# Splitting a product off the end of a recurrence block and running it in the first slots of the attention block behind it

## What is computed

```python
x = _layernorm(x + _L0_attn_ref(...))      # local attention and class token
x = _layernorm(x + _L0_xattn_ref(...))     # causal and cross attention
x = _layernorm(x + _L0_ffn_ref(...))       # expert choice, 16 experts
x = _layernorm(x + _L1_attn_ref(...))      # recurrence, then a gated feed-forward
x = _layernorm(x + _L1_xattn_ref(x, ctx, ctx, ...))  # cross attention, 16 heads
x = _layernorm(x + _L1_ffn_ref(...))       # top 2 of 8 experts

# the end of _L1_attn_ref, x being the residual behind the recurrence:
xn2 = _rmsnorm(x, g_ffn)
hid = _linear(xn2, w_fc, b_fc) * _silu(_linear(xn2, w_fcact, b_fcact))   # 128 -> 512
return x + _linear(hid, w_out, b_out)                                     # 512 -> 128
```

## Time and profile before

| | us |
|---|---|
| three runs | 580.11, 572.04, 574.46 |
| their median | 574.46 |
| the profiled execution, time of the run | 571.62 |
| the same execution, span from first to last instruction | 569.9 |

### The profile page before, as it was taken

One profiled execution on the slowest core, in us unless ns is written; L12 is line 12 of the kernel. 1 busy time (PEld: TensorE's weight loads), 2 busy tenths in 40 slices (PEclk: granted clock), 3 DMA queues, 4 the chain that ended last, 5 costly groups with the idle time before them and its releaser, 6 DMA issues. The chain is left out here.

```text
span 569.9 us, 10425 instructions
## 1 busy us (share of the span) xinstructions
PE 470.7 (83%) x3785; PEld 232.4 (41%) x3832; DVE 372.7 (65%) x868; ACT 223.3 (39%) x451; POOL 186.6 (33%) x310
## 2 busy tenths in 40 slices
PE   3899899988979889885069998697799888999993
PEld 2445444433334333332026986254233333444441
DVE  7555766877677677823996474854478784466574
ACT  1313444445754656673002122332114667624220
POOL 7752639467344471333200005720542100000000
PEclk9999999989998999998579999899699999999998
DMA  7230103054441220007013040000321100250700
GB/s 240 72 96 12 49 2 104 21 178 138 144 106 49 58 56 3 2 3 294 0 39 112 2 168 2 0 1 1 85 56 37 48 3 3 67 157 2 222 18 19
DMA packets 26900, 38.03 MB, mean 67 GB/s; under 512 B 3649, under 2 KB 19521, under 8 KB 26465
## 3 DMA queue, kind: packets, MB, share of 16 engines
q1 hardware_dynamic: 26848, 37.36, 21.8%
HBM read 23.91 MB, written 0.59 MB: 43 GB/s over the span
## 5 line engine op out<-in xcount | busy, mean ns | idle before, releaser
L1093 DVE TENSOR_REDUCE nmax<-bank 128x2 f32<-128x512 f32 (+2 forms) x240 | 144.4, 624 | 79.6 <-PE bank L862 37.9
L974 ACT ACTIVATE arena<-bank 128x512 f32<-128x512 f32 (+2 forms) x256 | 130.9, 526 | 122.6 <-PE bank L866 84.7
L862 PE MATMUL bank<-arena 62*128 62x256 bf16 (+2 forms) x512 | 86.0, 257 | 11.8 <-DVE nmax L1093 5.0
L504 PE MATMUL bank<-causal_qk,identb 128*128 128x512 bf16 x232 | 71.1, 402 | 26.1 <-DVE moe_top L1436 16.0
L866 PE MATMUL bank<-arena 64*128 64x256 bf16 (+2 forms) x512 | 85.8, 256 | 2.2 <-ACT arena L974 1.5
L907 PE MATMUL bank<-arena 128*32 128x256 f32 (+4 forms) x1088 | 73.0, 347 | 9.3 <-POOL arena L729 2.8
L862 PEld LDWEIGHTS bank<-arena 62*128 62x128 bf16 x512 | 29.8, 94 | 77.5 <-issue 46.6
L504 PEld LDWEIGHTS bank<-causal_qk,identb 128*128 128x128 bf16 x275 | 23.8, 104 | 55.7 <-DVE moe_top L1436 15.7
L729 POOL TENSOR_SCALAR_AFFINE_SELECT arena<-arena 128x256 f32<-128x256 f32 x64 | 25.6, 410 | 48.8 <-ACT arena L974 48.0
L866 PEld LDWEIGHTS bank<-arena 64*128 64x128 bf16 x512 | 30.3, 94 | 16.6 <-ACT arena L974 6.5
L907 PEld LDWEIGHTS bank<-arena 128*32 128x32 f32 x1088 | 21.4, 109 | 34.2 <-issue 19.1
(11 more groups left out here) (296 smaller groups left out, 813.5 us busy)
## 6 DMA issues: line engine op xcount, KB each, us to landing
arena<-arena SPq DMA_DIRECT2D x96, 128.0 KB, 2.4
fcw<-in_fc1T SPq DMA_DIRECT2D x16, 256.0 KB, 3.3
arena<-in_fc2T SPq DMA_DIRECT2D x1, 4096.0 KB, 12.5
arena<-comb_rows SPq DMA_DIRECT2D x16, 256.0 KB, 4.3
fcw<-in_last SPq DMA_DIRECT2D x1, 2304.0 KB, 8.3
arena<-pos_rows SPq DMA_DIRECT2D x16, 128.0 KB, 3.0
arena<-comb_rows SPq DMA_DIRECT2D x16, 128.0 KB, 4.3
w<-in_w SPq DMA_DIRECT2D x1, 1216.0 KB, 6.1
```

The lines of the kernel that those rows point to most:

```text
L504: nc.tensor.matmul(bank[:, :], m.identb[:, :], m.causal_qk[:, 0:4, :], start=True, stop=True)
L862: mins = t.matmul(mout[:, i, :], stack_rows(m, nm, h0 + i, 0, MAX_ROWS)[:, qt * P:(qt + 1) * P], stack_rows(m, nm, h0 + i, 1, MAX_ROWS)[:, ...
L974: s.activation(m.prob[h % 8][:, 0:w], score_bank(n, h)[:, 0:w], ACT.Exp).then_inc(exps, 1)
L1093: v.tensor_reduce(m.nmax[n % 2][:, qt, h0:h0 + nh], MX[c % NMX][:, 0:nh * (k1 - k0)].rearrange("p (h k) -> p h k", h=nh), AX.X, ALU.max, n ...
```

## The change

The product of the second half leaves the recurrence. `product_first` stands behind unit 4 in place of `product(0)` behind unit 5. DVE takes the sum and the statistics of the first half behind `hidden(4)` (`spread_first`), its norm behind `hidden(5)` (`norm_first`), and `hidden(6)` and `hidden(7)` last. The transposes of the first half go into bank 0 instead of bank 2. The table of Exp is loaded in the attention block, in slot 4. `hid[1]` moves to columns 12288 to 14335 of `arena`, where it survives into the attention block. There `LastNorm` issues the product of the second half on PE in slot 1, DVE's sum and statistics in slot 4 instead of 0 (behind `split_first`), POOL's power in slot 6 instead of 1, DVE's norm in slot 9 instead of 4, and PE's transposes in slot 14 instead of 10, so that ACT copies them in slot 15 instead of 11.

```diff
-S_NORMED, S_NEEDED = 10, 32 - PRE
+S_PRODUCT, S_SUMMED, S_POWER, S_NORM, S_NORMED, S_NEEDED = 1, 4, 6, 9, 14, 32 - PRE
...
-    hid = [a[:, 14336:16384].rearrange("p (f t) -> p f t", f=FT), a[:, 8192:10240].rearrange("p (f t) -> p f t", f=FT)]
+    hid = [a[:, 14336:16384].rearrange("p (f t) -> p f t", f=FT), a[:, 12288:14336].rearrange("p (f t) -> p f t", f=FT)]
...
         unit(4)
+        product_first()
         unit(5)
-        product(0)
         unit(6)
         unit(7)
-        product(1)
         pe.wait_ge(zf, 1)
         for i in range(4):
-            ins = t.transpose(B[2][:, i * P:(i + 1) * P], m.x[1][:, i, :], m.ident[:, :])
+            ins = t.transpose(B[0][:, i * P:(i + 1) * P], m.x[1][:, i, :], m.ident[:, :])
...
-        act.wait_ge(neg, 3)
-        s.activation(table[:, :], ndt[:, :], ACT.Exp).then_inc(neg, 1)
...
-        for u in range(1, 2 * FT):
+        for u in range(1, FT + 1):
             hidden(u)
+        spread_first()
+        hidden(FT + 1)
         norm_first()
+        for u in range(FT + 2, 2 * FT):
+            hidden(u)
...
     def gpsimd(self, pool, slot):
         m = self.m
-        if slot == 1:
+        if slot == S_POWER:
             pool.wait_ge(self.var_ready, 1)
...
     def tensor(self, pe, slot):
         m = self.m
+        if slot == S_PRODUCT:
+            for i in range(4):
+                for f in range(FT):
+                    ins = self.nc.tensor.matmul(m.bank[1][:, i * D:(i + 1) * D], self.hid[:, f, i * P:(i + 1) * P],
+                                                m.w_out[:, f, :], start=(f == 0), stop=(f == FT - 1))
+            ins.then_inc(self.out_mm, 1)
...
     def scalar(self, act, slot):
         m = self.m
+        if slot == S_SUMMED:
+            self.nc.scalar.activation(self.table[:, :], m.eps[:, 0:1], ACT.Exp).then_inc(self.exp_in, 1)
...
-        if slot == 0:
+        if slot == S_SUMMED:
+            dve.wait_ge(self.out_mm, 1)
...
-        if slot == S_SPLIT + 1:
+        if slot == S_NORM:
             dve.wait_ge(self.rstd_ready, 1)
```

More of the change, by code:

```diff
@@ L1102, in layer0_attention @@
         rec = recurrence(nc, m, dram, ctx)
+        m.late_hid = rec.hid[1]
         choice = expert_choice(nc, m, dram, ctx, rec)
@@ L1588, in recurrence @@
     scaled_in, factors, zeroed = sem("scaled_in"), sem("factors"), sem("zeroed")
-    part.xn_ready = xn_ready
+    part.xn_ready, part.hid = xn_ready, hid
     def tiles(c):
@@ L1662, in unit, with product_first @@
             t.matmul(B[k + 1][:, :], m.w_act[:, f * P:(f + 1) * P], xnT[:, cols(c)], start=True, stop=True).then_inc(ffn_mm, 1)
-        def product(c):
-            pe.wait_ge(hid_in, FT * (c + 1))
+        def product_first():
+            pe.wait_ge(hid_in, FT)
             for i in range(4):
                 for f in range(FT):
-                    ins = t.matmul(B[c][:, i * D:(i + 1) * D], hid[c][:, f, i * P:(i + 1) * P],
+                    ins = t.matmul(B[0][:, i * D:(i + 1) * D], hid[0][:, f, i * P:(i + 1) * P],
                                    m.w_out[:, f, :], start=(f == 0), stop=(f == FT - 1))
@@ L1734, in scalar_on @@
             silu(u)
-        act.wait_ge(neg, 3)
-        s.activation(table[:, :], ndt[:, :], ACT.Exp).then_inc(neg, 1)
         act.wait_ge(xt_mm, 1)
-        s.copy(m.xT[1][:, cols(0)], B[2][:, :]).then_inc(xt_in, 1)
+        s.copy(m.xT[1][:, cols(0)], B[0][:, :]).then_inc(xt_in, 1)
     def vector_on(dve):
@@ L1798, in norm_first @@
             v.tensor_scalar(m.veps[:, tiles(0)], m.mv[:, tiles(0), 1], LN_EPS, None, ALU.add).then_inc(var_ready, 1)
+        def norm_first():
             dve.wait_ge(rstd_ready, 1)
@@ L1827, with __init__ @@
 class LastNorm:
-    def __init__(self, nc, m):
-        self.nc, self.m = nc, m
+    def __init__(self, nc, m, hid):
+        self.nc, self.m, self.hid = nc, m, hid
+        self.table = m.sb("late_table", [P, 1])
         sem = lambda n: m.ctx.enter_context(nc.semaphore("late_" + n))
         self.uses = [(S_NORMED, "normed", 0)]
-        self.var_ready, self.rstd_ready, self.z_ready = sem("var_ready"), sem("rstd_ready"), sem("z_ready")
+        self.var_ready, self.rstd_ready, self.z_ready, self.out_mm, self.exp_in = [sem(n) for n in (
+            "var_ready", "rstd_ready", "z_ready", "out_mm", "exp_in")]
     def sync(self, sp, slot):
@@ L2204, in build @@
         router = Router(nc, m, last, ctx)
-        layer1_cross(nc, m, router, LastNorm(nc, m), Top2(nc, m, last, router))
+        layer1_cross(nc, m, router, LastNorm(nc, m, m.late_hid), Top2(nc, m, last, router))
 def kernel(**inputs):
```

2 lines of the change are left out of this document (1 added, 1 removed).

## The result

The changed kernel takes 572.12 us in the median (569.55 to 577.81, 20 runs), the kernel before 574.81 us (571.52 to 580.73, 20 runs). The ratio of the two is 0.9954 with a 95% interval of 0.9932 to 0.9976: 0.46% or 2.6 us faster, between 1.4 and 3.9 us. The profiled execution of the changed kernel has a span of 567.8 us instead of 569.9, which is 2.1 us less. In the terms of the prediction this is "within 2%", with a gain that is nevertheless clear.

What follows compares the result with a forecast made beforehand. The prediction took the wait chain through PE's late-half transposes to bound the kernel. 6.35 us gained ahead of t0, less 2.65 + 1.65 = 4.3 lost behind it, left about 2.05 us: 571.0 us, range 567.0 to 575.5.

Steps and rivals of the forecast that it cites:

- the footing: Base time for the gain: between the profiled execution (571.62 us) and the median shown (574.46), giving a forecast of 571.0 us.
- Ahead of t0: End of the recurrence: earlier first-half product and norm bring the attention block forward from 396.95 to 390.6 us, 6.35 us gained.
- t0: Start of the first product of the attention block on PE; 396.95 us in the kernel before.
- The split: DVE's split in the attention block, now ahead of the sum: ends at t0 + 5.5 us, clear of POOL's residual.
- The product behind t0: Second half's product on PE in the attention block: starts at t0 + 1.14, takes 3.84 us, ends at t0 + 4.98.
- The norm: DVE's four late-half tile norms: each waits for about one POOL instruction, 3.15 us instead of 1.50, 1.65 us lost.
- its upper end: Norm's worst case: POOL waits as well, a whole POOL instruction lies between any two norms, 2.4 us lost.
- Transposes: PE's transposes of the late half: start at t0 + 12.55 us; 8.24 us behind it before.
- The clock, costed at nothing: PE's clock around transposes and fillers: no change if it rises at the same filler, otherwise about 2 us either way.
- the clear norm: Rival: the late half's norm meets no POOL instruction; loss 2.65 us, gain 3.7 us, 569.3 us; chance 0.25.
- the gain absorbed: Rival: something else holds the first maxima, such as stacking DMAs or a later wait; gain 0, 573 us; chance 0.1.
- The slow product: Rival: clock falls at the seam, the moved product takes 7.5 instead of 3.84 us; 1.1 us loss, 574.1 us; chance 0.15.

Runs made afterwards that it cites:

- The run with the late product: The changed kernel with the second half's product behind the queries of job 1 (slot 10) instead of in slot 1; ratio to the kernel before 0.9990.
- the run in which POOL waits: The changed kernel, but POOL waits for the late half's norm before the residual of job 0 and split of job 1; ratio to the kernel before 0.9936.
- the one in which only the residual meets the norm: The changed kernel with the late half's transposes in slot 10 instead of 14, ACT's copy ahead of job 1's high part; ratio to the kernel before 0.9937.
- the run that left one of 6.83 us: The changed kernel, but DVE does all eight hidden blocks first and the first half's statistics and norm last; ratio to the kernel before 1.0165.
- the run with few fillers: The changed kernel with 2 fillers instead of 16 on PE between the late half's transposes and the first maximum; ratio to the kernel before 1.0236.

## Why the prediction was right

The forecast was 2.05 us of gain, at 571.0 us with a range of 567.0 to 575.5. The stretch at the seam shrank by 2.07 us, and the time by 2.6 us (1.4 to 3.9) to 572.12 us. Every step of the sum was found at its place; what was luck is said with the clock and the footing.

- *Ahead of t0.* Predicted 390.6 us, found 390.76. The product, DVE's statistics (2.6 us), the power and the norm follow at the forecast distances. `hidden(5)` fitted into DVE's gap (0.54 us of idle time were left), and the table of Exp is hidden in both places.
- *The split.* Its third step (L994) of 1.21 us takes 0.68 us now that POOL's residual is out of its way, as forecast.
- *The product behind t0.* It ends 391.99 + 3.84 - 390.76 = 5.07 us behind t0 (forecast 4.98), the sum starts at 5.40. The run with the late product shows that the slack was indeed a few tenths of a microsecond.
- *The norm.* Forecast 3.15 us, found 3.19, by the mechanism named: the run in which POOL waits and the one in which only the residual meets the norm gave 1.49 and 2.00 us for the same instructions. (The terms that the prediction lists add up to 3.13 us, and those of its upper end to 2.45 us; both roundings are without weight.) The Trainium skill ("SBUF — State Buffer", section "SBUF: two separate sides") states an exclusive lock between GpSimd and DVE, where DVE's instruction uses two ports or has two inputs in SBUF: whichever starts first has it for its whole instruction, and the other is blocked. That each norm ends 0.1 us behind a POOL instruction agrees with it; that the first norm was held although its record starts 0.04 us ahead of POOL's (399.89 and 399.93 us) does not. Taken as the prediction did for its upper end, with a POOL instruction between every two norms and POOL waiting too, the rule would have given 3.9 us, and the row has 3.19. POOL's own instructions were not lengthened in this place (0.72 and 1.16 us). In the kernel before, POOL's residual took 0.87 us beside DVE's split, so that POOL too is sometimes held can't be excluded.
- *Transposes.* Forecast 12.55 us behind t0, found 12.52.
- *The clock, costed at nothing.* From the start of the transposes to the first maximum it took 6.03 us, before 6.14. That this came out near nothing was luck: over the runs in which the clock was low there, the same instructions took 5.34 (the run in which POOL waits) to 6.89 us (the late product), and 4.02 us with the clock up. The prediction's 2 us less were right in size; of its 2 us more, 0.75 were seen.

The rivals: the clear norm did not occur (3.19 us), nor was the gain absorbed (158.6 and 158.5 us behind the first maximum). The slow product did not occur in this kernel, where PE had holes of 0.30 and 1.12 us ahead of t0; it occurred in the run that left one of 6.83 us. What the prediction put too low was the footing: 571.0 us stood between the profiled execution and the median of three, while the median over 20 runs is 574.81 us before, 2.7 us above the changed kernel's 572.12. That step was a guess about the spread of executions, and that the forecast is off by only 1.1 us is in part its luck.

## What to carry to other kernels

Work that the next stage doesn't need first can cross a seam, but that gains nothing by itself: find the wait that ends the stage and reorder for that, since the product's leaving alone cost 4.6 us here. And try the reordering alone first, as its estimate here came to about the whole gain. When a step moves, look at what now runs at the same time on the engine beside it, not only at its own length: four small norms took twice as long because another queue had been freed. And where PE idles for several microseconds ahead of fillers meant to raise its clock, put the fillers into the hole. Sixteen of them fitted into idle time here, what followed ran fast at once, and all but two of the old ones could go.

## What was not expected of the hardware

In the run with few fillers PE was busy without a hole for some 44 us and yet kept the granted clock of 0.50, most of it in slots that consist of two fillers of 128x512 and two products with 62 rows; in the same slots it kept 1.00 when the stretch had begun there. It rose between 457.5 and 460 us (0.68 in that window), 8 to 10 us after the slots had changed to other products without fillers (from 449.4 us on). Whether that change brought it up was not tried.

The spread of 1.5% between executions of one kernel lies at least partly in where the clock falls. Ahead of all edits the same 12 projection records took 5.32 us in four of the ten profiled executions (one of them that of the kernel before) and 7.01 us in the other six. In the changed kernel the granted clock was 1.00 all through them; in the run in which POOL waits it was 0.72, 0.50 and 0.92 in their first three windows of 2 us. From their start to the end of unit 4 the four needed 26.7 to 27.9 us and the six 30.4 to 30.8. What decides it in a given execution stays open.
